# A graph transformer's kernel: gelu units computed before the gates in a dense expert layer, and the scaling of graph attention's exponentials on VectorE instead of GpSimd

## The reference, cut to what matters

```python
probs  = softmax(xn @ gate_w.T)                  # 625 x 8
g      = best two of probs, over their sum + 1e-9, else 0
hidden = gelu(xn @ w1[e] + b1[e])                # 8 experts of 192: 1536 in all
x     += sum_e g[:, e] * (hidden_e @ w2[e] + b2[e])
```

```python
e     = leaky_relu(a_src[src] + a_dst[dst], 0.2)
ex    = exp(e - segment_max(e, dst)[dst])
alpha = ex / (segment_sum(ex, dst)[dst] + 1e-16)
out   = segment_sum(alpha[:, :, None] * h[src], dst)
```

## Time and profile before

| | us |
|---|---|
| median of 3 runs (2091.84 to 2098.1) | 2092.32 |
| the profiled execution | 2091.71 |
| its span, first to last instruction | 2089.8 |
| layer norm ahead of the dense experts ends | 470.8 |
| dense experts: first matmul of a hidden unit | 503.4 |
| dense experts: first matmul with the second weights | 546.6 |
| dense experts end | 660.4 |
| graph attention, first layer's 40 units | 850 to 1050 |

### The profile page before, as it was taken

How to read it: one execution, slowest core, us unless ns; L and a number is a source line. 1 busy time by engine, 2 the same in 40 slices (tenths; PEclk the granted TensorE clock), 3 DMA queues, 4 the chain that set the end, 5 groups by cost and what they waited for, 6 DMA issues and landing times.

```text
span 2089.8 us, 30875 instructions
## 1 busy us (share of the span) xinstructions
PE 1883.1 (90%) x12246; PEld 1788.8 (86%) x12247; DVE 1306.9 (63%) x2404; ACT 909.6 (44%) x1497; POOL 219.7 (11%) x169
## 2 busy tenths in 40 slices
PE   5988998978997999488757999999999999999998
PEld 4876888977887999488747999999999999999998
DVE  6997766442335544888866575355656666667786
ACT  2331213312222542566733323334555655666776
POOL 0000000003000001565710000000010101000010
PEclk9998999997999999689979999999999999999999
DMA  3110002100111311100022112125565756676895
GB/s 111 46 46 1 24 27 95 54 1 24 69 46 45 106 54 49 64 19 21 16 106 71 53 63 98 69 100 213 190 208 197 234 207 227 245 246 231 284 319 205
DMA packets 36795, 234.29 MB, mean 112 GB/s; under 512 B 5916, under 2 KB 7318, under 8 KB 14632
## 3 DMA queue, kind: packets, MB, share of 16 engines
q1 hardware_dynamic: 31318, 217.41, 29.3%
q0 software_dynamic: 2656, 8.99, 1.9%
q10 hardware_dynamic: 2674, 5.87, 0.7%
HBM read 221.91 MB, written 10.35 MB: 111 GB/s over the span
## 4 chain that ended last, share of the span: by engine, by line
PE 75%; DVE 13%; issue 8%; ACT 2%; DMA 2%; POOL 1%; SPq 0%; DVEq 0%; POOLq 0%; ACTq 0%
PE bank L313 16%; PE bank L315 15%; PE bank L314 15%; PE bank L2441 8%; PE bank L570 4%; PE bank L2442 3%; PE bank L2453 3%; DVE weight_lo L286 2%; PE bank L2457 2%; PE bank L2445 2%; PE bank L2454 2%; PE bank L2456 1%; DVE mix_kv L793 1%; PE bank L2444 1%; DVE gat_unread L2034 1%
## 5 line engine op out<-in xcount | busy, mean ns | idle before, releaser
L286 DVE TENSOR_TENSOR weight_lo<-weight_raw,weight_hi 128x2304 fp32r<-128x2304 f32 (+1 forms) x155 | 389.9, 2519 | 36.7 <-ACT weight_hi L276 36.5
L276 ACT ACTIVATE weight_hi<-weight_raw 128x2304 fp32r<-128x2304 f32 (+1 forms) x155 | 323.3, 2087 | 92.2 <-DMA weight_raw<-in_ffn_w 52.0
L313 PE MATMUL bank<-xT_hi,weight_hi 128*128 128x306 f32 (+1 forms) x576 | 183.8, 319 | 4.0 <-issue 2.0
L314 PE MATMUL bank<-xT_lo,weight_hi 128*128 128x306 f32 (+1 forms) x576 | 178.8, 310 | 0.0
L315 PE MATMUL bank<-xT_hi,weight_lo 128*128 128x306 f32 (+1 forms) x576 | 178.5, 310 | 0.0
L313 PE MATMUL bank<-weight_hi,xT_hi 128*128 128x384 f32 (+1 forms) x480 | 160.2, 334 | 9.3 <-DVE xT_lo L334 4.5
L2815 DVE TENSOR_TENSOR hidden_tmp<-hidden_tmp,bank 128x160 f32<-128x160 f32 (+5 forms) x192 | 65.7, 342 | 160.3 <-ACT hidden_tmp L2601 160.3
L315 PE MATMUL bank<-weight_hi,xT_lo 128*128 128x384 f32 (+1 forms) x480 | 156.8, 327 | 0.0
L314 PE MATMUL bank<-weight_lo,xT_hi 128*128 128x384 f32 (+1 forms) x480 | 156.8, 327 | 0.0
L570 PE MATMUL bank<-one_hot_dst,one_hot_src 125*128 125x313 f16 x800 | 122.8, 305 | 15.2 <-ACT packed_counts L584 7.9
L313 PE MATMUL bank<-weight_hi,hidden_hi 128*128 128x384 f32 (+1 forms) x366 | 124.6, 340 | 0.9 <-DVE weight_lo L286 0.9
(11 more groups left out here) (491 smaller groups left out, 5178.5 us busy)
## 6 DMA issues: line engine op xcount, KB each, us to landing
weight_raw<-in_ffn_w SPq DMA_DIRECT2D x111, 1152.0 KB, 5.2
weight_raw_fifth<-in_ffn_w SPq DMA_DIRECT2D x25, 1152.0 KB, 5.3
weight_raw<-in_shared_w SPq DMA_DIRECT2D x16, 1152.0 KB, 5.2
weight_raw<-in_mix_kv SPq DMA_DIRECT2D x8, 1152.0 KB, 7.1
weight_raw<-in_gat_w SPq DMA_DIRECT2D x8, 768.0 KB, 4.9
weight_raw<-in_mix_q SPq DMA_DIRECT2D x4, 1152.0 KB, 5.1
weight_raw<-in_mix_out SPq DMA_DIRECT2D x4, 1152.0 KB, 5.2
weight_raw<-in_gnn_w SPq DMA_DIRECT2D x4, 1152.0 KB, 5.4
```

The costliest lines, as they stand in the source:

```text
L276: act.activation(upper_, whole_, ACT.Copy).then_inc(*w_hi.one())
L286: dve.tensor_tensor(lower_, whole_, upper_.bitcast(F32), ALU.subtract).then_inc(*w_lo.one())
L313: pe.matmul(dst, a[0], b[0], start=first, stop=False)
L314: pe.matmul(dst, a[0], b[1], start=False, stop=False)
```

## The change

In the dense experts `tmp` is replaced by `acted`, which has a place for each of a half's 12 units and lies in the memory of `hT`'s lower part. PE does units 0 and 1, then the logits in another form (8 gate columns as the weights, 320 tokens moving, 36 matmuls in two banks), unit 2, the transposition of the logits (5 small transposes into one bank), units 3, 4 and 5, the counts' and the gates' transpositions, unit 6, and then the spreading of the gates for units 0 to 6 in a row; from unit 7 on each unit is followed by its own as before. ACT makes gelu of units 0 to 5 as they come, among its copies, and multiplication and split of units 0 to 6 follow when the gates are there; the weights' chunk 3 is split ahead of unit 6's gelu instead of after unit 5's. The blanking of `hT`'s unused columns is gone, and the last tile has 114 rows in place of 128.

In graph attention POOL keeps the terms alone. DVE takes up each unit at lag 3 by itself: add, reciprocal, and one TENSOR_SCALAR over 128 by 640 that multiplies by the reciprocal and by `has_edge`.

```diff
         def tensor():
-            logits_tensor(gp, logit_banks, xT_ready)
-            pe.wait_ge(*count_f_made.at(TT))
...
+            hidden(0)
+            hidden(1)
+            logits()
+            hidden(2)
+            logits_turned()
+            hidden(3)
+            hidden(4)
+            hidden(5)
+            counts_turned()
             gates_tensor(gates, gate_banks)
+            hidden(6)
             pe.wait_ge(*gT_lo_made.at(TT))
             pe.wait_ge(*sel_made.at(1))
+            for i in range(EARLY):
+                picked(i)
             for kh in range(2):
...
+                for i in range(max(EARLY, 12 * kh), 12 * (kh + 1)):
+                    hidden(i)
+                    picked(i)
...
         def scalar():
+            def hidden(i):
+                hid, k, span, n = unit(i)
+                act.wait_ge(*hid_full.at(i + 1))
+                if i >= 12:
+                    act.wait_ge(*y_full.at(2 * TT))
+                act.activation(acted[:, k, span], hid_banks[i][:, 0:n], ACT.Gelu, bias=b1[:, hid:hid + 1]).then_inc(*gelu.one())
...
             gates_scalar(gT, gate_banks)
...
+            weight_read[c0] = hid_full.at(6)
+            weights_hi(c0)
+            hidden(6)
+            for i in range(EARLY):
+                hidden_upper(i)
...
         def vector():
+            def hidden(i):
+                _, k, span, n = unit(i)
+                dve.wait_ge(*gelu.at(i + 1))
+                dve.wait_ge(*pick_full.at(i + 1))
+                dve.tensor_tensor(acted[:, k, span], acted[:, k, span], pick_banks[i][:, 0:n], ALU.mult).then_inc(*gated.one())
+                dve.wait_ge(*gated.now())
+                dve.wait_ge(*h_hi.at(i + 1))
+                lower(at(hT, ALL, k, span), acted[:, k, span]).then_inc(*h_lo.one())
...
+            gates_vector(gT, gate_banks)
+            weights_lo(c0)
             dve.wait_ge(*x_ready)
...
-            for i in range(N1 + 4):
-                u = unit(i, 0)
-                if u is not None:
-                    terms(u, *units[u][0:3])
-                q = pair_closing(i, 3)
-                if q is not None:
-                    grp, h, t0, n = pairs_of[q]
-                    for a in range(n):
-                        u = FIRST_OF[q] + a
-                        e = edge_w[:, u % ZS, :]
-                        pool.wait_ge(*e_norm.at(q + 1))
-                        pool.tensor_tensor(e, e, total[:, grp % 2, h, t0 + a:t0 + a + 1].broadcast_to([P, TP]), ALU.mult).then_inc(*e_scaled.one())
+            for u in range(N1):
+                terms(u, *units[u][0:3])
...
-                q = pair_closing(i, 3)
-                if q is not None:
-                    grp, h, t0, n = pairs_of[q]
-                    tot = total[:, grp % 2, h, t0:t0 + n]
-                    dve.wait_ge(*e_exp.at(FIRST_OF[q] + n))
+                u = unit(i, 3)
+                if u is not None:
+                    grp, h, t = units[u][0:3]
+                    e = edge_w[:, u % ZS, :]
+                    tot = total[:, grp % 2, h, t:t + 1]
+                    dve.wait_ge(*e_exp.at(u + 1))
                     own_step(dve.tensor_scalar(tot, tot, 1e-16, None, ALU.add))
                     own_step(dve.reciprocal(tot, tot))
-                    dve.tensor_tensor(tot, tot, has_edge[:, t0:t0 + n], ALU.mult).then_inc(*e_norm.one())
+                    dve.tensor_scalar(e, e, tot, has_edge[:, t:t + 1], ALU.mult, ALU.mult).then_inc(*e_scaled.one())
```

176 lines of the change are left out of this document (91 added, 85 removed).

## The result

| | before | after |
|---|---|---|
| median | 2093.3 us (4 runs, 2091.8 to 2098.1) | 2056.6 us (4 runs, 2054.0 to 2059.6) |
| profiled execution | 2091.7 | 2056.3 |
| its span | 2089.8 | 2054.2 |

The ratio is 0.9821, with a 95% interval from 0.980 to 0.984: **36.7 us faster**. I had predicted 2069.6 and a range down to 2060.

A forecast was written before the change was run, and what follows sets the result against it. PE, busy 90%, was taken to bound the kernel, with DVE the fullest engine in graph attention. 2092.3 - 22.7 (dense experts) + 0 (graph attention, between -8 and +8) = 2069.6 us, range 2060 to 2081.

The forecast's parts named there:

- The last wait, DVE's backlog: Dense experts, ahead of the second weights: PE waits 2.6 us instead of 1.64, since DVE's seven waiting units are still felt.
- Port: Dense experts: POOL's marking of empty edges holds DVE operations on the shared SBUF port, costing 1 us, between 0 and 4.
- Rival (d): Dense experts: the early units run at half clock, 22.4 us more, so 2092 and no change; chance 0.03.
- The bound that I had set, 24: Dense experts: the largest gain allowed, 24 us, if the port never holds and the counts are quick.
- the replay of the turns: Graph attention: DVE's turns from 947 to 968 replayed with the new prices; the sum over the run is 0.
- the relief: Graph attention: port fights taken from DVE, 7.6 us at the peak and 9.4 at the rest of z, 17 us.
- the small steps of before: Graph attention: DVE's small steps per pair before the change, priced 24 x 0.46 = 11.0 us, against 12.0 after.
- +0.87 for each group: Graph attention, preparing turns: half of the scaling lies on the chain, +0.87 us for each of 3 groups, +2.6.
- PE's waits for the pair's scaling: Graph attention: PE's seven later waits for POOL, 7.9 us, go but mostly return as waits for DVE; -2 taken.
- (a): Graph attention: the scaling is never held and PE waits less, -12 us, so 2057.6; chance 0.10.
- (b): Graph attention: DVE becomes the bound, all 0.54 us per turn on the chain in 40 turns, +15, 2084.6; chance 0.10.
- (c): Graph attention: each scaling is held for a whole term of 1.55 us, 66 us over 40 turns, 2136; chance 0.03.

The follow-up runs named there:

- the dense part alone: The kernel before with only the diff's parts outside graph attention, graph attention left as before: 2067.1 us (ratio 0.9871).
- the late marking: The changed kernel, but GpSimd marks empty edges after the first half's units and VectorE adds the marks in the second half's first sum: 2055.8 us (0.9829).
- the pairwise kernel: The changed kernel, but VectorE scales both units of a pair when the second one's exponentials are there, same instructions per unit: 2057.2 us (0.9827).
- the extra instruction: The changed kernel plus one unneeded GpSimd addition, 128 by 320 in SBUF, behind each of the 40 terms: 2065.4 us (0.9875).
- five early units: The changed kernel with five units ahead of the spreading of the gates instead of seven, chunk 3's split back behind unit 5: 2059.0 us (0.9836).

## Why the prediction was right or wrong

**Dense experts, 22.7 predicted, 26.2 in the trace, 25.7 by the runs.** The mechanism was right in the main: the early units at full clock, the gates' chain covered, the counts' copies on ACT as the limit between. The last wait, DVE's backlog, was right with the dense part alone (2.8); in the profiled execution PE's own last unit set it, as shown above. What was off are sizes, all in one direction:
- Six units took 15.8, not 16.7. I took the unit's 2.84 from the earlier trace rows, where a spreading of gates follows each. The six that have none behind them take 2.5 to 2.7 (2.53 from 473.47 to 476.00).
- Logits 5.3 in place of 5.7, their turn 0.4 in place of 0.7, and the start 0.1 earlier. With the units, the counts come 1.8 before the forecast.
- From there to unit 6 it is 3.5 in place of 3.9: ACT's copies of the counts go at 0.34, not 0.41. Seven spreadings in a row take 2.2, not 3.4; 0.48 was the price of one between two units.
- Port: 0.6 in place of 1. The rest, from the counts' start to the last product, is 28.1 in place of 28.8 + 1.
Together 3.5. My wait of PE, 2.6 to 4, holds for the dense part alone (2.8) and not for the late marking (2.2) nor for the profiled execution (1.7), and the product started 49.6 us behind the norm, where I had given 52 to 54. Rival (d), early units at half clock, did not come: 1.00 up to 501.4. The bound that I had set, 24, was too near: I had varied the port and the counts, not the units' pace, on which 16.7 of the 53 us rested.

**Graph attention, 0 predicted, 8.4 in the trace, 11.4 by the runs.** The step that failed is the replay of the turns ("the sum over the run is 0"). I had replayed the turns from 947 to 968, whole ones from peak 19 to 24, and took their prices for the run:

```profile
948.60:966.66 18.06, 14.17 (x105) 13.55 (x104) 16.83 (x38) 14.18 (x34) 15.92 (x10) 0.97 0.00 1
...
967.66 1.64 DVE L334 TENSOR_TENSOR gat_zT_lo<-gat_z,gat_zT_hi 128x128 fp32r<-128x128 f32 x1
```

```profile
918.55:936.56 18.01, 16.64 (x113) 15.87 (x112) 15.99 (x43) 13.94 (x33) 7.92 (x5) 0.92 0.00 0
...
937.31 0.28 DVE L334 TENSOR_TENSOR gat_zT_lo<-gat_z,gat_zT_hi 128x128 fp32r<-128x128 f32 x1
```

The first rows are peaks 19 to 24, before and after: 18.06 and 18.01, no gain indeed. But that stretch was a short one by chance: the same five turns in the other two tens took 19.08 and 19.08 before (19.1 to 19.3 in all three tens with the dense part alone) and 18.02 after. And the turns on both sides, of which the replay had at most an end, gave the most: peak 18 to 19 went from 4.25 to 3.47, and peak 24 to 25 from 7.40 to 5.02 (6.03 and 5.81 to 5.01 in the other tens). In that last turn lies the rest of z over 128 columns, the second rows. The prices missed in both directions, too: from the end of one peak to the end of the next, turns with z's rest took 2.84 and 2.86, not 3.35, and the one without 2.81, not 3.0; the one with four additions to x took 5.09, not 4.4, and the one that had been held for 1.57 took 4.42, where 1.5 less than before is 3.3. Two terms of the relief were wrong in size:
- I priced the small steps of before at their free times, 24 x 0.46 = 11.0. They took 21.0, since in 13 of the 24 pairs the addition or the product met an instruction of GpSimd. The row that would have told it was in the same view as the earlier trace rows; I had even quoted one such addition, 1.00 in place of 0.14, and used it only as evidence.
- z's rest: I counted the 15 of 256 columns (9.4 of loss) and not the six of 128 columns (6.8 before, 1.7 after, 5.1). And I left some of both in the turns; in fact they fell from 22.2 to 9.4.

So the relief was 27.5 us, not 17 and what the replay kept of it. On the other side the scaling cost 29.2, more than the 20.4. Of the difference 4.1 is the size, since its time does not shrink in proportion to the columns: it takes 0.61 free for 640 columns, where 768 took 0.68. The other 4.7 are holds. My price with a hold, about 0.9, fits (0.93 in the mean of the 15 held ones), but 25 of 40 were free, and the mean is 0.73. DVE's total came out as I had it, unchanged. But a total of zero is not a time of zero. From the first peak to the last the time fell by 6.8: by 8.7 in the turns without preparation, by 2.1 at the fill's first five and the last four, and it rose by 4.0 in the turns with preparation (-1.2, +2.6 and +2.6). I had given +0.87 for each group of the latter; whether that price was wrong the traces don't tell, since the clock differs there. PE's waits for the pair's scaling, of which I took 2 of 7.9, were no separate gain that the runs tell: the pairwise kernel has the pairs' timing and the same time. The 40 units took 191.3 us, just below the 192 to 208 that I had given.

**The rivals.** (a), port freed, was the right direction: -12 against 8.4 to 11.4. Its reason, that the scaling is never held, was wrong; it is held in 15 of 40 units, and the gain comes from what GpSimd's *second* instruction no longer holds. (b) and (c) did not come. The price of (c), a whole hold per turn, needs a scaling that starts with a term; the held ones start 0.95 to 1.3 behind it, but for those of the fill, two of which start 0.16 behind it and take 1.73 and 1.75.

**The port.** I had set the rule of the Trainium skill (SBUF — State Buffer, "SBUF: two separate sides"), a hold for the whole instruction, against a row of the marking, and took the row for the marking alone; in graph attention I had a hold up to the term's end, which is the rule. For GpSimd's f32 TENSOR_TENSOR the trace agrees with the Trainium skill: all 15 scalings of the changed kernel that began over 0.2 us before a term's end ended 0.34 to 0.36 behind it, and the extra instruction shows the same in both directions. Most of these holds are short: seven of the 15 scalings take 0.66 to 0.69 us, five 0.77 to 0.96, and only three, in the fill, over 1. The Trainium skill (same section) names as concerned, on DVE's side, an instruction with two inputs in SBUF or one in a mode that uses both ports. The rows fit: z's rest, the peak, the small product and the scaling are held, and lower parts that read a bank (0.88 for two, beside a term or not) are not. For the marking, a TENSOR_SCALAR on 16-bit data, the price was 0.6 in all, where 5.8 came out by the rule of the Trainium skill, and here the measurement decides. Why that instruction holds so little no run shows.

## What to carry to other kernels

When an engine is relieved of a partner on a shared port, price every small instruction that stands beside the partner by its mean in the trace, not by its free time: 24 times three steps of 0.14 to 0.16 us hid 10 us here. Replay turns from more than one period, and all kinds of them: the five that I took were the ones that gained nothing. A balance of busy time that comes to zero says nothing of the time; ask of each term in which turns it lies, those that wait or those that are full. A step ahead of a wait can lie in it where the same step behind it is added to it: moving the scaling of 12 units by one place cost 6 us of the 11 that they take. And before a longer stretch is put down to an engine's work, look at PE's clock in it.

## What the runs showed of the hardware

- GpSimd's f32 TENSOR_TENSOR in SBUF and the DVE instructions named above exclude each other for whole instructions, whichever began first. A held one ends by a fixed tail behind the other's end: 0.35 us for the scaling of 640 columns, which takes 0.61 free, and 0.72 to 0.74 for the GpSimd addition of 320 columns behind a scaling, which takes 0.85 to 0.89 free. Beside GpSimd's TENSOR_SCALAR on 16-bit data the holds were 0.33 and 0.27 us in 12.4 us of it. Taking work away ahead of such a hold gained nothing (a start 0.19 earlier, a duration 0.19 longer).
- A DVE addition over 128 by 2 columns was held until the term's end (495 ns in the mean of 16), the same over 128 by 1 never (143 ns in the mean of 40). A product of two inputs in SBUF was held over one column too (376 ns in the mean of 39).
- A TENSOR_SCALAR with two scalars per row takes 0.61 us for 640 columns and 0.68 for 768: about 0.28 fixed and 0.5 ns per column, an estimate from these two points.
- PE's granted clock was 0.54 for 3.7 us in the middle of dense work that had run at 1.00 for 30 us without a gap, and the unit in it took 1.5 us longer. The traces of the dense part alone and of five early units have no dip there but one at 522.5 and 522.7, just behind PE's wait, where the first tile with the second weights takes 4.9 us in place of 3.4; that of the late marking has none in the stretch. What starts it no run shows. Single traces of a stage differ by 1 to 3 us through such dips, which is why the parts are priced by medians here.
